# A fused cross-attention and ternary feed-forward kernel: the opening in another order

## The reference

```
x = x + attention(layernorm(x), ctx, mask)       # scores / sqrt(512), masked softmax, readout of ctx
x = x + ffn(layernorm(x))
ffn(y) = linear(silu(linear(y, w1, g1)) * linear(y, w2, g2), w3, g3)
linear(v, w, g):
    r  = g * v * rsqrt(mean(v*v) + 1e-8)
    s  = 127 / clip(max|r|, 1e-4)                # per row
    xq = clip(round(r * s), -128, 127) / s
    a  = mean|w|                                 # one number per weight matrix
    wq = round(tanh(w / (a + 1e-8))) * arctanh(a)
    return xq @ wq.T
```

## Time and profile before

| | |
|---|---|
| median of three runs | 445.47 us (444.27 to 445.84) |
| profiled execution | 444.06 us |
| its span | 442.3 us |
| PE busy | 398.4 us, 90% |
| DVE busy | 382.3 us, 86% |
| POOL busy | 358.3 us, 81% |
| ACT busy | 343.5 us, 78% |
| mean granted TensorE clock | 0.954 of 2.4 GHz |

### The profile page before, as it was taken

One profiled execution on the slowest core, in us unless ns is written; L12 is line 12 of the kernel. 1 busy time (PEld: TensorE's weight loads), 2 busy tenths in 40 slices (PEclk: granted clock), 3 DMA queues, 4 the chain that ended last, 5 costly groups with the idle time before them and its releaser, 6 DMA issues.

```text
span 442.3 us, 8289 instructions
## 1 busy us (share of the span) xinstructions
PE 398.4 (90%) x1870; PEld 179.0 (40%) x1870; DVE 382.3 (86%) x835; ACT 343.5 (78%) x618; POOL 358.3 (81%) x559
## 2 busy tenths in 40 slices
PE   8326596899999999999999999999999989999996
PEld 8102232334434443444344444444344443444443
DVE  5599598999799979997999979997999799798794
ACT  3677779687998789886998698878988697667661
POOL 0149888999889988898879987998889897899970
PEclk9755796999999999999999999999999999999999
DMA  6999881545675547843684568554784425354541
GB/s 256 398 333 367 282 189 24 143 90 125 171 194 103 119 105 188 184 103 81 170 194 92 117 168 189 105 119 102 183 185 103 88 66 113 80 96 101 106 103 73
DMA packets 110359, 66.40 MB, mean 150 GB/s; under 512 B 100736, under 2 KB 100864, under 8 KB 106752
## 3 DMA queue, kind: packets, MB, share of 16 engines
q1 hardware_dynamic: 110336, 66.14, 58.5%
HBM read 33.10 MB, written 8.39 MB: 94 GB/s over the span
## 4 chain that ended last, share of the span: by engine, by line
PE 53%; POOL 13%; DVE 12%; ACT 10%; issue 9%; DVEq 1%; DMA 1%; POOLq 0%; SPq 0%; ACTq 0%
PE S L1279 29%; PE DN L1312 15%; POOL stageB L549 5%; PE R L1258 3%; ACT stageB L740 3%; DVE stageB L972 3%; ACT prob L695 2%; DVE hm L978 2%; POOL c L538 2%; ACT L695 2%; PE DN L1320 1%; DVE ga L945 1%; PE R L1225 1%; ACT junk_x L718 1%; ACT sg L748 1%
## 5 line engine op out<-in xcount | busy, mean ns | idle before, releaser
L549 POOL TENSOR_TENSOR stageB<-stageB,g3b 128x512 f32<-128x512 f32 x127 | 161.9, 1289 | 7.4 <-DVE stageB L972 4.8
L1279 PE MATMUL S<-W2q,q12T 128*128 128x512 f16 x512 | 134.2, 385 | 5.3 <-DVE W2q L1044 3.3
L1279 PE MATMUL S<-W1q,q12T 128*128 128x512 f16 x512 | 135.9, 389 | 1.2 <-ACT sg L748 0.9
L1312 PE MATMUL DN<-W3q,stageB 128*128 128x512 f16 x496 | 122.2, 380 | 0.5 <-DVE W3q L1044 0.4
L748 ACT ACTIVATE sg<-S,asc 128x512 f32<-128x512 f32 x128 | 86.9, 682 | 25.5 <-PE S L1279 23.4
L972 DVE TENSOR_TENSOR stageB<-sg,S 128x512 f32<-128x512 f32 x128 | 86.1, 678 | 20.0 <-ACT sg L748 20.0
L978 DVE TENSOR_REDUCE hm<-stageB 128x1 f32<-128x512 f32 x127 | 85.9, 677 | 2.0 <-POOL stageB L549 1.9
L1279 PEld LDWEIGHTS S<-W2q,q12T 128*128 128x128 f16 x512 | 50.4, 99 | 69.4 <-DVE W2q L1044 4.5
L1279 PEld LDWEIGHTS S<-W1q,q12T 128*128 128x128 f16 x512 | 48.8, 100 | 70.2 <-issue 9.2
L1312 PEld LDWEIGHTS DN<-W3q,stageB 128*128 128x128 f16 x496 | 47.9, 98 | 59.1 <-issue 1.1
L755 ACT ACTIVATE junk<-stageB 128x1024 bf16<-128x1024 f32 x64 | 67.3, 1051 | 4.3 <-DVE stageB L972 4.2
(11 more groups left out here) (127 smaller groups left out, 431.1 us busy)
## 6 DMA issues: line engine op xcount, KB each, us to landing
X<-in_x SPq DMA_DIRECT2D x8, 1024.0 KB, 6.3
out_x<-X SPq DMA_DIRECT2D x32, 256.0 KB, 2.7
xTs<-in_xT SPq DMA_DIRECT2D x7, 1024.0 KB, 7.2
X<-in_w1T SPq DMA_DIRECT2D x4, 1024.0 KB, 10.7
stageB<-in_w2T SPq DMA_DIRECT2D x4, 1024.0 KB, 18.5
X<-in_w3T SPq DMA_DIRECT2D x4, 1024.0 KB, 9.2
ctxr<-in_ctx SPq DMA_DIRECT2D x16, 128.0 KB, 3.0
ctxc<-in_ctx SPq DMA_DIRECT2D x8, 128.0 KB, 4.4
```

Of the source, the lines that this page charges most:

```text
L549: nc.gpsimd.tensor_tensor(gh[q][:, part], hp[:, part], g3b[:, part], ALU.mult).then_inc(s_gh_made, 1)
L1279: mm = nc.tensor.matmul(bank[n % 2][:, :], q12T[q][:, i * KD + k, :], w[:, n, k, :], start=(k == 0), stop=(k == KD - 1))
L1312: mm = nc.tensor.matmul(bank[:, :], src[:, k, :], W3q[:, k, :], start=(k == 0), stop=(k == KH - 1))
```

## The change

Five instruction lists are reordered, and three operations change engine or are new.

- The scaling of W1's last part moves from ACT to POOL (and SP's load of W3's last part waits for POOL instead of ACT).
- The sum of W3's part 2 moves from DVE to ACT, so ACT does all four.
- ACT's logarithms are split otherwise: W1's alone, then W2's and W3's together (before W1's and W2's together, then W3's). The Ln table of the first is loaded before W1 is scaled.
- POOL makes W1's constant before it quantizes row 0.
- DVE does W1's last half sum ahead of row 0's gain, W2's mean and first clip ahead of row 1's preparation, and `attention_x1(0,1)`, which gives rows 2 and 3, after gate(0,2).
- PE runs fourteen products of 128 x 128 ones between the readout of batch 0 and W2's total, into a bank that is free then; `up(2, 0)` stands before the attention products of batch 1, and slot(2) leaves it out.
- SP issues context 1 earlier, x and its transposed copy of batch 1 after W3.

```diff
# SP
             load_ctxc(1)
+            load_ctxr(1)
             transpose_12(0, 0)
...
             load_w(stageA, w3T, 0, w_in[2][0])
-            load_ctxr(1)
             sp.wait_ge(s_w1_act, 2)
             load_w(stageA, w3T, 1, w_in[2][1])
-            load_xT(1)
-            transpose_12(1, 1)
             sp.wait_ge(s_w1_pool, 1)
             load_w(stageA, w3T, 2, w_in[2][2])
+            sp.wait_ge(s_w1_pool, 2)
+            load_w(stageA, w3T, 3, w_in[2][3])
+            transpose_12(1, 1)
             load_x(1)
-            sp.wait_ge(s_w1_act, 3)
-            load_w(stageA, w3T, 3, w_in[2][3])
+            load_xT(1)
# POOL
             stage_a_mean(1, 1)
+            arctanh_series(0)
+            arctanh_choice(0, 1)
             quantize_12(0)
-            arctanh_series(0)
+            stage_a_worth_gate(0)
             weight_scale(0, stageA, W1f, 2, s_w1_pool)
+            weight_scale(0, stageA, W1f, 3, s_w1_pool)
             stage_a_root(1, 1)
-            arctanh_choice(0, 1)
-            stage_a_worth_gate(0)
             weight_scale(1, stageB[:, :], W2f, 3, s_w2_pool)
-            stage_a_mean(2, 2)
             quantize_12(1)
-            arctanh_series(1)
-            stage_a_mean(3, 3)
             stage_a_worth_gate(1)
...
# ACT
+            table(1, ACT.Ln)
+            logs(0, 1, 1)
             weight_scale(0, stageA, W1f, 0, s_w1_act)
             weight_scale(0, stageA, W1f, 1, s_w1_act)
...
-            table(1, ACT.Ln)
-            logs(0, 2, 1)
+            table(2, ACT.Silu)
             weight_scale(1, stageB[:, :], W2f, 1, s_w2_act)
-            table(2, ACT.Silu)
             weight_scale(1, stageB[:, :], W2f, 2, s_w2_act)
             silu(0, 0, 0)
-            weight_scale(0, stageA, W1f, 3, s_w1_act)
...
# PE
             attention_readout(0, 1)
+            for i in range(14):
+                nc.tensor.matmul(xP[0][:, 0:P], ones[:, :], ones[:, :], start=True, stop=True)
             weight_total(1, s_w2_abs, WC + 1)
...
+            up(2, 0, 0)
             attention_probT(1)
             attention_readout(1, 0)
...
-                up(t, 0, q)
+                if later(t, 3):
+                    up(t, 0, q)
```

More of the change, by code:

```diff
@@ L625, in _ @@
             gain_3(0, 0, 0)
+            gain_3(0, 1, 0)
+            stage_a_mean(2, 2)
+            gain_3(0, 2, 0)
+            arctanh_series(1)
+            gain_3(0, 3, 0)
             stage_a_root(2, 2)
-            gain_3(0, 1, 0)
-            gain_3(0, 2, 0)
+            gain_3(1, 0, 1)
             quantize_12(2)
-            gain_3(0, 3, 0)
-            arctanh_choice(1, 1)
+            stage_a_mean(3, 3)
+            gain_3(1, 1, 1)
+            attention(1)
+            weight_scale(2, stageA, W3f, 2, s_w3_pool)
+            arctanh_choice(1, 2)
             stage_a_worth_value(0)
-            stage_a_root(3, 3)
-            attention(1)
+            stage_h_root(0, 0)
             stage_a_worth_value(1)
-            gain_3(1, 0, 1)
-            gain_3(1, 1, 1)
+            gain_3(1, 2, 1)
             stage_a_worth(2, 2)
-            stage_h_root(0, 0)
             arctanh_series(2)
             arctanh_choice(2, 2)
-            weight_scale(2, stageA, W3f, 2, s_w3_pool)
-            gain_3(1, 2, 1)
+            stage_a_root(3, 3)
             def slot(b, j, last=False, attn=False, prep=False):
@@ L807, in _ @@
             weight_abs(2, stageA, 1, s_w3_abs)
+            silu(0, 3, 0)
+            stage_a_var(2)
+            weight_abs(2, stageA, 2, s_w3_abs)
+            silu(1, 0, 1)
+            square(0, 0)
             attention_ccT(1)
-            silu(0, 3, 0)
-            square(0, 0)
-            silu(1, 0, 1)
-            stage_a_var(3)
             weight_abs(2, stageA, 3, s_w3_abs)
             silu(1, 1, 1)
-            attention_half(1)
             square(0, 1)
@@ L818, in _ @@
             weight_scale(2, stageA, W3f, 0, s_w3_act)
+            attention_half(1)
             silu(1, 3, 1)
+            weight_scale(2, stageA, W3f, 3, s_w3_act)
+            logs(1, 3, 2)
             attention_exp(1)
-            weight_scale(2, stageA, W3f, 3, s_w3_act)
+            stage_a_var(3)
+            quantize_3(0, 0, 0)
             attention_probT(1)
-            quantize_3(0, 0, 0)
-            logs(2, 3, 2)
             square(1, 0)
+            table(3, ACT.Silu)
             quantize_3(0, 1, 0)
-            table(3, ACT.Silu)
             def slot(b, j, last=False, attn=False, prep=False):
@@ L1064, in _ @@
             attention_x1(0, 0)
+            weight_abs(0, stageA, 3, s_w1_abs, WN // 2)
             dve.wait_ge(s_gains_in, 32)
             stage_a_gain(0)
[L1067 removed]
             weight_mean(0, WC + 1)
@@ L1082, in _ @@
             weight_clip(W1f, 1, s_w1_act, 2, s_w1_q)
             weight_clip(W2f, 1, s_w2_act, 1, s_w2_q)
+            stage_a_gain(1)
+            stage_a_max(1, 1)
+            stage_a_factor(1, 1)
+            gate(0, 0)
             weight_clip(W1f, 2, s_w1_pool, 1, s_w1_q)
             weight_clip(W2f, 2, s_w2_act, 2, s_w2_q)
-            gate(0, 0)
-            stage_a_gain(2)
-            weight_clip(W1f, 3, s_w1_act, 3, s_w1_q)
-            stage_a_max(2, 2)
-            attention_cc(1)
+            gate(0, 1)
@@ L1091, in _ @@
+            weight_clip(W1f, 3, s_w1_pool, 2, s_w1_q)
             weight_clip(W2f, 3, s_w2_pool, 1, s_w2_q)
-            gate(0, 1)
-            stage_a_factor(2, 2)
             gate(0, 2)
+            attention_x1(0, 1)
             max_3(0, 0, 0)
             gate(0, 3)
-            weight_abs(2, stageA, 2, s_w3_abs)
+            attention_cc(1)
+            max_3(0, 1, 0)
+            stage_a_gain(2)
+            gate(1, 0)
+            max_3(0, 2, 0)
+            stage_a_max(2, 2)
+            gate(1, 1)
@@ L1098, in _ @@
+            weight_mean(2, WC)
+            stage_a_factor(2, 2)
+            max_3(0, 3, 0)
+            gate(1, 2)
             attention_xstat(1)
-            gate(1, 0)
-            weight_mean(2, WC)
-            max_3(0, 1, 0)
-            gate(1, 1)
+            gate(1, 3)
+            stage_h_top(0)
             attention_softmax(1)
-            max_3(0, 2, 0)
-            gate(1, 2)
-            max_3(0, 3, 0)
+            weight_scale(2, stageA, W3f, 1, s_w3_dve)
+            max_3(1, 0, 1)
@@ L1107, in _ @@
             weight_clip(W3f, 0, s_w3_act, 1, s_w3_q)
[L1108 to L1117 removed]
             weight_clip(W3f, 1, s_w3_dve, 1, s_w3_q)
             max_3(1, 1, 1)
+            stage_h_factor(0, 0)
             weight_clip(W3f, 2, s_w3_pool, 1, s_w3_q)
+            weight_clip(W3f, 3, s_w3_act, 2, s_w3_q)
@@ L1121, in _ @@
+            attention_norm(1)
+            stage_a_gain(3)
+            attention_x1(1, 0)
+            stage_a_max(3, 3)
             max_3(1, 2, 1)
-            weight_clip(W3f, 3, s_w3_act, 2, s_w3_q)
+            stage_a_factor(3, 3)
             dve.wait_ge(s_coef_ready, 3)
```

24 lines of the change are left out of this document (4 added, 20 removed).

## The result

The changed kernel takes 446.67 us (median of 7 runs, 446.56 to 447.42) against 444.34 us (443.99 to 445.84) in the runs of before that share its chip: a ratio of 1.0049, 95% interval 1.0034 to 1.0064. It is 2.3 us slower where 2.7 us faster was forecast. The executions profiled took 447.09 us (span 445.1) and 444.06 us (span 442.3). A second set of runs gave the same: 446.67 us, 1.0047 (1.0024 to 1.0070). Two executions that took far longer than the rest, 608 us of before and 694 us of e17, are left out of every median and ratio.

What follows compares the result with a forecast made beforehand. POOL's queue up to `quantize_12(3)` was taken to set when the even part starts. 4.9 - 2.0 - 1.5 + 1.3 = 2.7 us earlier, against a runs' median of 445.47, gave 442.8 us, range 439.0 to 447.0.

Steps and rivals of the forecast that it cites:

- What bounds the kernel: Opening: the even part starts as early as POOL reaches `quantize_12(3)`, 55.8 us after it started `quantize_12(0)`.
- every row from there as far apart as now: Rows from `stage_a_mean(4)` on: expected to keep their distances, with `stage_a_mean(4)` itself at 81 to 82 us.
- Part 1: POOL's start: W1's series before `quantize_12(0)` fills its wait from 23.75 us; 4.9 us gained, bounds 4.0 and 5.2.
- Part 2: W1's last scaling, moved from ScalarE to POOL: 2.0 us of POOL's queue lost, up to 3.0 with a clash.
- Part 3: Waits POOL newly meets after 29.5 us, mostly for DVE's statistics of x: 1.5 us lost, bounds 0 and 5.5.
- Part 4: Clashes in which POOL or DVE stands while the other runs: 1.3 us gained, bounds -1.5 and +3.
- Part 5: Edits costed at nothing: filler products (done by 31.3 us), W3's sum on ScalarE, `up(2,0)` earlier, SP's order.
- Rival (a): Transfers decide: row 1's transpose queues behind W3, up(1,0) starts late; slower, 449.8 us at 184 GB/s; chance 0.15.
- Rival (c): DVE and POOL miss each other more: relief 3, waits 0.5, 5.4 us gained, 440.1 us; chance 0.20.
- Rival (b): POOL swaps one delay for another: 4.9 - 3.0 - 4.0 + 1.3 = -0.8, 446.3 us at worst; chance 0.27.
- tests given for being wrong: POOL waiting over 4 us between 28 and 80, up(1,0) after 51 us, or silu(2,1) not following row 4's mean.

Runs made afterwards that it cites:

- e17: Kernel before with only two lines of POOL's list exchanged, `arctanh_series(0)` ahead of `quantize_12(0)`: 442.38 us, ratio 0.9952.
- e18: e17 with W1's last scaling also on POOL, behind the one before it: 443.35 us, ratio 0.9979 to the kernel before.
- e7: Changed kernel with W1's last scaling back on ScalarE behind silu(0,0): 446.30 us, ratio 1.0042 to the kernel before.
- e12: Changed kernel without the fourteen products of ones on TensorE: 446.10 us, ratio 1.0048 to the kernel before.
- e4: Changed kernel with row 1's preparation moved early, its factor ahead of the clips on DVE: 445.98 us, ratio 1.0042 to the kernel before.
- e13: Kernel before with the fourteen products of ones added ahead of W2's total and nothing else: 444.40 us, ratio 1.0001.
- e14: Changed kernel with `up(2,0)` back at the head of the first slot: 446.95 us, ratio 1.0054 to the kernel before.

## Why the prediction was wrong

- **What bounds the kernel: right.** The opening's end on POOL sets the start of the even part: ScalarE's step waits 4.4 us for mark 4, `silu(2,1)` follows at 86.50, and from mark 8 on the rows keep their distance. What failed is "every row from there as far apart as now": the four rows behind mark 4 cost 0.93 us.
- **Part 1, POOL starts 4.9 us sooner: right.** Before, `quantize_12(0)` came 8.25 us behind mark 0, now the series comes 3.38 behind it: 4.87 us. The forecast for `quantize_12(0)`, 28.0, came as 28.54.
- **Part 2, 2.0 us lost to W1's last scaling: right in length (3.92 for two), wrong as a loss of the opening.** e18 and e7 show that it fills time in which POOL waits: 0.14 us on the path in the one, and in the other 2.1 us of waiting in its place. The medians of e17 and e18 leave a cost in time open.
- **Part 3, the waits, is the step that failed: 1.5 us forecast, 5.36 measured** (3.88, 0.54, 0.94). Its 1.1 for the statistics was right (0.94). Its "without a wait" for `quantize_12(1)` was not, for three reasons. (1) W2's last part is taken up at 33.17 and not at the 30.87 that I carried over from a kernel whose other transfers and products were different (1.8 us later when measured from mark 0). So the mean came at 35.5 and not at 33.3. (2) POOL's W2 scaling went ahead of the clips; I had named this case and its end, POOL waiting until 43.4 (row 1's factor starts at 43.40), but counted it as a bound; that the number fits is luck, since the mean was 2.2 us later than in that case. (3) The mean in time would not have been enough: in e12 it is there at 33.62 and POOL still waits 3.2 us, since row 1's factor stands behind the clips on DVE. e4 takes that away, and POOL waits for the gate and row 2's step instead.
- **Part 4, relief: 1.3 forecast, 1.65 by the balance.** Mark 0 to `quantize_12(3)` grew from 64.04 to 64.84 us, and 4.87 - 1.96 - 5.36 leaves 1.65 for that; it is what the other terms do not explain, not a measurement of the clashes.
- **Part 5, "at nothing": wrong for the products.** They ended in time, as worked out (29.6, before 31.3). Their price came another way, with the landing: 1.1 us of opening in e12, of which the medians show 0.6, not clear of noise. What `up(2,0)` taken forward is worth stays open.
- **Rival (a) fell,** though its sign was met. `up(1,0)` starts at 51.45, past the 51 given. But row 1's transpose was issued at 46.32, when the quantization was through, landed 3.1 us later, and PE was busy with row 0 without a break up to 51.45: `up(0,2)` had waited 3.4 us for a clip, and `up(0,2)` and most of `up(0,3)` ran at the slower level. (Its price was also off in itself: 5.25 MB at 184 GB/s are 28.5 us, which puts the landing near 60 and not at 56.)
- **Rival (c) fell. Rival (b), one delay for another, was the mechanism.** That its worst sum (-0.8) is also the measured one (-0.80) is luck: its terms were 3.0, 4.0 and 1.3 where 1.96, 5.36 and 1.65 came. With the 0.93 us that no case had, it became a loss.
- **The range.** 446.67 us lies within 439.0 to 447.0, but that range was counted from 445.47 us, where the seven runs of before have 444.34; and the bounds of parts 3 and 4, taken together, reach 4.1 us of loss, 449.6.

Two of the tests given for being wrong were met: over 4 us of POOL's waits between 28 and 80 (5.4), and `up(1,0)` after 51 us.

The sum added pieces of POOL's queue as if POOL alone set its pace. What DVE had to do next decided how much of the early start was kept. e17 shows what the idea is worth alone, 1.7 us of opening and about 2 us of time. The rest of the change, which was to help it, costs 2.5 us of opening (64.68 against 62.19) and 0.93 us behind it.

## What to carry to other kernels

When a change starts an engine sooner, follow the engine that feeds it just as far: a gain at the head of a queue is worth only what the feeding engine's next pieces allow, and its list must not be loaded at the same place. Make the exchange alone before the new order around it; here the two lines were the gain and the rest the loss. And a landing time read from a trace holds for that kernel's other traffic only; ask which cover the kernel had that made a late landing harmless.

## What the runs showed of the hardware that was not expected

- Small products on TensorE, whose operands lie on the chip, go with a later landing of a transfer in flight: 0.7 to 1.1 us in one pair of kernels (e13 against before), 1.8 in another (e12 against after). With them a load of program code (0.02 MB on queue 8) falls into the transfer, which it does not without them; that it is the cause was not tested.
- The filler products of after raised the granted clock (1.00 in 30 to 33 us, 0.50 there in e12). They ended at 29.56, PE was idle for 4.9 us, and the first products of row 0, from 35.33, ran at the slower level (1.86 and 1.89 us a group). In e13 the idle time was 2.8 us and the first group took 1.02 us; the next, behind 4.6 us of idle time, took 1.89.
- Where a clip or a subtraction of DVE met an operation of POOL that was running, it ended 0.55 us (the clip of 38.47) and 0.28 us behind it, while one that started near the boundary of two operations of POOL took 0.47 us. So 0.6 us of shift decides: the same subtraction took 0.47 and 1.07 us, and PE waited 0.62 us longer for it.
- Kernels whose lists are the same up to there (after and e14) had `up(1,2)` at the faster level in one execution and at the slower in the other, and the opening with the slower was up to 0.85 us longer. A difference of less than that between the openings of two kernels needs TensorE's rows beside it.
- DVE had 0.46 us of idle time between two of its own operations, at the same instruction in every kernel of one family and in none of the other; empty instructions ahead of it moved it by nothing.
